# Two layers of a graph network on one core: where the graph attention begins, where its weights are split, and the order of its sums and second scores

## The reference

```python
xn = layernorm(x)
# attention branch, 12 heads of 64: q = elu(q)+1, k = elu(k)+1
attn = q @ k.T ; attn /= sum(attn) ; out = (attn @ v) @ w_proj + b_proj
# graph branch, twice: gat_layer(x, W, att_src, att_dst, bias, heads, out_ch)
h = (x @ W.T).reshape(n, heads, out_ch)
a_src, a_dst = (h * att_src).sum(-1), (h * att_dst).sum(-1)
e = leaky_relu(a_src[src] + a_dst[dst], 0.2)
alpha = softmax of e over the edges that end in the same node
out = segment_sum(alpha * h[src], dst) + bias
# first: 8 heads of 128, then relu; second: 1 head of 768
x = x + graph branch + attention branch
```

## Time and profile before

| | us |
|---|---|
| median of 3 runs | 2029.58 (2028.18 to 2029.92) |
| the profiled execution | 2031.99 |
| its span in the trace | 2030.1 |
| PE busy in the span | 1864.3 (92%) |
| DVE busy | 1307.8 (64%) |
| ACT busy | 907.4 (45%) |
| POOL busy | 154.9 (8%) |
| linear projection | 739.0 to 777.1 |
| graph attention, first product to last sum | 776.8 to 1065.2 |

### The profile page before, as it was taken

One profiled execution on the slowest core, in us unless ns is written; L12 is line 12 of the kernel. 1 busy time (PEld: TensorE's weight loads), 2 busy tenths in 40 slices (PEclk: granted clock), 3 DMA queues, 4 the chain that ended last, 5 costly groups with the idle time before them and its releaser, 6 DMA issues.

```text
span 2030.1 us, 30857 instructions
## 1 busy us (share of the span) xinstructions
PE 1864.3 (92%) x12197; PEld 1769.5 (87%) x12198; DVE 1307.8 (64%) x2466; ACT 907.4 (45%) x1503; POOL 154.9 (8%) x129
## 2 busy tenths in 40 slices
PE   5987999899999996888768999999999999999998
PEld 4875888898889995788667899999999999999998
DVE  6997766545345655987765663446565666666886
ACT  2331222324134433765434223235555665666775
POOL 0000000004000003422110000000101001001010
PEclk9997998999999997888979899999999999999999
DMA  3110002001212202010012112236566657676795
GB/s 114 48 47 1 24 24 102 32 24 49 70 48 86 71 32 96 22 37 16 34 76 97 61 66 101 86 117 220 198 216 199 225 210 243 226 258 236 286 321 197
DMA packets 36796, 234.30 MB, mean 115 GB/s; under 512 B 5916, under 2 KB 7318, under 8 KB 14632
## 3 DMA queue, kind: packets, MB, share of 16 engines
q1 hardware_dynamic: 31318, 217.41, 30.1%
q0 software_dynamic: 2656, 8.99, 2.0%
q10 hardware_dynamic: 2674, 5.87, 0.7%
...
## 4 chain that ended last, share of the span: by engine, by line
PE 74%; DVE 13%; issue 8%; ACT 3%; DMA 2%; POOL 0%; SPq 0%; DVEq 0%; ACTq 0%; POOLq 0%
PE bank L326 16%; PE bank L327 15%; PE bank L328 15%; PE bank L2599 8%; PE bank L650 4%; PE bank L2600 3%; PE bank L2611 3%; DVE weight_lo L299 2%; PE bank L2615 2%; PE bank L2603 2%; PE bank L2612 2%; PE bank L2614 1%; DVE mix_kv L873 1%; PE bank L2602 1%; DVE gat_edge L2243 1%
## 5 line engine op out<-in xcount | busy, mean ns | idle before, releaser
L299 DVE TENSOR_TENSOR weight_lo<-weight_raw,weight_hi 128x2304 fp32r<-128x2304 f32 (+1 forms) x155 | 388.8, 2513 | 38.7 <-ACT weight_hi L289 38.5
L289 ACT ACTIVATE weight_hi<-weight_raw 128x2304 fp32r<-128x2304 f32 (+1 forms) x155 | 323.2, 2087 | 71.6 <-DMA weight_raw<-in_ffn_w 50.4
L326 PE MATMUL bank<-xT_hi,weight_hi 128*128 128x320 f32 (+1 forms) x576 | 182.0, 316 | 2.2 <-DVE xT_lo L347 2.1
L327 PE MATMUL bank<-xT_lo,weight_hi 128*128 128x320 f32 (+1 forms) x576 | 177.5, 308 | 0.0
L328 PE MATMUL bank<-xT_hi,weight_lo 128*128 128x320 f32 (+1 forms) x576 | 177.3, 308 | 0.0
L326 PE MATMUL bank<-weight_hi,xT_hi 128*128 128x384 f32 (+1 forms) x480 | 162.5, 339 | 8.3 <-DVE xT_lo L347 4.8
L2973 DVE TENSOR_TENSOR hidden_tmp<-hidden_tmp,bank 128x160 f32<-128x160 f32 (+5 forms) x192 | 65.6, 341 | 160.8 <-ACT hidden_tmp L2759 160.0
L327 PE MATMUL bank<-weight_lo,xT_hi 128*128 128x384 f32 (+1 forms) x480 | 158.7, 331 | 0.0
L328 PE MATMUL bank<-weight_hi,xT_lo 128*128 128x384 f32 (+1 forms) x480 | 158.5, 330 | 0.0
L650 PE MATMUL bank<-one_hot_dst,one_hot_src 125*128 125x313 f16 x800 | 122.6, 304 | 15.2 <-ACT packed_counts L664 7.9
L2759 ACT ACTIVATE hidden_tmp<-bank,ffn_b_by_load 128x160 f32<-128x160 f32 (+5 forms) x192 | 73.4, 402 | 121.4 <-PE bank L2603 115.2
...
## 6 DMA issues: line engine op xcount, KB each, us to landing
...
```

The lines of the kernel that those rows point to most:

```text
L289: act.activation(upper_, whole_, ACT.Copy).then_inc(*w_hi.one())
L299: dve.tensor_tensor(lower_, whole_, upper_.bitcast(F32), ALU.subtract).then_inc(*w_lo.one())
L326: pe.matmul(dst, a[0], b[0], start=first, stop=False)
L327: pe.matmul(dst, a[0], b[1], start=False, stop=False)
```

## The change

- `normalised_attention` ends after the attends. All ten are made before any projection: group 0's beside the last four query products, group 1's after them. Its output tiles get room for all five node tiles, and turns, projections and their sums are returned as functions (`Projection`) that the graph attention calls.
- `graph_attention` starts when the attends are done (`attended`). In each engine's list the steps of group 0 and the turns, products, halves and sums of the projection alternate. The edge buffers 0 to 4 lie in memory that the attends have freed, 5 and 6 in that of the projection's operands. ACT's wait for the last sum and the store of x stand in tick 5; the projection's halves and sums of the last tiles stand in ticks 2, 3 and 5.
- Of the stage's weights one is split before the loop; six are split one at a time at the end of the ticks 10, 12, 14, 20, 24 and 28 (`SPLIT`). SP loads one weight fewer before the stage.
- On DVE, a tick's sums come behind the lower halves of the turned edges, scaling and peak. Second scores of a pair's first tile follow its sums in the same tick, the second tile's come in the next tick behind these as well. The lower halves of h2 are made after the loop, two ahead of the score rows' lower halves and three behind.

```diff
-        kp = pair("mix1_k", [P, TT, HALF], scope)
-        vp = pair("mix1_v", [P, TT, HG, DO], scope)
...
         inverse = sb("mix1_inverse", [P, 2, HG], F32, scope)
+
+        row2 = sb("mix1_row", [P, (GAT_FIRST - 4 * (2 * PAIRS * (TP + PW) + WORK * HALF + 2 * HG)) // 4], F32, scope)[:, 0:D]
+        kp = pair("mix1_k", [P, TT, HALF], scope)
+
+        with ExitStack() as outs_scope:
+            outs = sb("mix1_out", [P, TT, D], F32, outs_scope)
+        vp = pair("mix1_v", [P, TT, HG, DO], scope)
         blank = work[:, :, :].rearrange("p a n -> p (a n)")[:, 0:PAIRS * PW].rearrange("p (a n) -> p a n", a=PAIRS)
 
...
+        BESIDE = {8: (0,), 9: (1,), 10: (2,), 11: (3, 4)}
 
         def sync():
             sp.wait_ge(*x_ready)
             sp.dma_start(bias0[:, :], spread_row(ins["mix1_b"], D)).then_inc(*row_in.dma())
-            sp.dma_start(outs[:, 0, :], spread_row(ins["gat_b2"], D)).then_inc(*row_in.dma())
-            weights_load(c0 + 8 + DEPTH - 1)
+            sp.dma_start(row2, spread_row(ins["gat_b2"], D)).then_inc(*row_in.dma())
+            weights_load(c0 + 10)
 
...
+                end.then_inc(*o_full.one())
 
             keys(0)
             values(0)
...
             per_head(1)
-            attend(0)
-            attend(1)
-            turn(0)
+            for i in range(8, 12):
+                queries(i)
+                for t in BESIDE[i]:
+                    attend(0, t)
             for t in range(TT):
-                if t + 2 < TT:
-                    attend(t + 2)
-                project(t, 0)
-                if t + 1 < TT:
-                    turn(t + 1)
-                project(t, 1)
+                attend(1, t)
 
 
         def scalar():
...
             biases()
             values(0)
             weights_lo(c0 + 1)
-            queries(0)
+            for i in range(6):
+                queries(i)
             per_head(0)
             weights_lo(c0 + 2)
             keys(1)
             weights_lo(c0 + 3)
             values(1)
             weights_lo(c0 + 4)
...
+        for engine in (act, dve, pool, sp):
+            engine.wait_ge(*projection.attended)
         (x_kept, x_back, b1_in, pick_filled, pick_made, log_made, terms_made, edges_known,
          att_in, h_full, h_hi, h_lo, scored, score_turned, score_hi, score_lo, rows_full, rows_kept,
          e_acted, e_made, e_exp, e_scaled, ex_turned, ex_hi, ex_lo, z_full, z_relu, z_hi, z_lo,
@@ -1843,22 +1855,25 @@
         minus_peak = sb("gat_minus_peak", [P, 2, 2, TT], F32, gat)
         total = sb("gat_total", [P, 2, 2, TT], F32, gat)
         rowT = pair("gat_rowT", [2, TP], gat)
-        hg = [pair(f"gat_h{n}", [P, TT, GW], gat) for n in range(2)]
-        src_row = [sb(f"gat_src_row{n}", [P, 2, TP], F32, gat) for n in range(2)]
...
+        dst_bias = sb("gat_dst_bias", [P, 2, TT, 2], F32, gat)
+        b1 = sb("gat_b1", [P, G1], F32, gat)
+        half_scores = sb("gat2_half_scores", [P, TT, 2, 2], F32, gat)
+        h_first = pair("gat_h0", [P, TT, GW], gat)
+        src_first = sb("gat_src_row0", [P, 2, TP], F32, gat)
+
         ZS, XS = 7, DEPTH
...
 
         PREPARE = {6: (0, 1), 7: (2, 3), 8: (4, "turned"), 9: ("spread",)}
 
+        SPLIT = {10: c0 + 2, 12: c0 + 3, 14: c0 + 4, 20: c0 + 5, 24: c0 + 6, 28: c0 + 7}
+
         def unit(i, lag):
 
...
             sp.dma_start(b1[:, :], ins["gat_b1"]).then_inc(*b1_in.dma())
             for grp in range(4):
                 cols = slice(grp * GW, (grp + 1) * GW)
-                if grp:
-                    sp.wait_ge(*scored.at(TT * grp))
-                else:
-                    sp.wait_ge(*x_ready)
+                sp.wait_ge(*(scored.at(TT * grp) if grp else projection.bias_added))
                 for n, name in enumerate(("gat_as1", "gat_ad1")):
                     sp.dma_start(att[:, n, :], spread_row(ins[name][cols], GW)).then_inc(*att_in.dma())
-                weights_load(c0 + 5 + grp)
+                if grp:
+                    weights_load(c0 + 5 + grp)
             sp.wait_ge(*scored.at(4 * TT))
             sp.wait_ge(*e_acted.at(30))
             sp.wait_ge(*terms_made.at(TT + 30))
...
+            def project(t):
+                projection.project(t, 0)
+                projection.project(t, 1)
+
+            prepare(0, 0)
+            projection.turn(0)
+            prepare(0, 1)
+            prepare(0, 2)
+            projection.turn(1)
+            prepare(0, 3)
+            prepare(0, 4)
+            projection.project(0, 0)
+            prepare(0, "turned")
+            projection.project(0, 1)
+            projection.turn(2)
+            projection.project(1, 0)
+            prepare(0, "spread")
+            projection.project(1, 1)
+            projection.turn(3)
+            project(2)
+            projection.turn(4)
+            project(3)
+            project(4)
             for i in range(N1 + LAST_LAG):
                 q = pair_closing(i, 9)
                 if q is not None and pairs_of[q][1] == 1:
...
 
 
         def scalar():
-            act.activation(edge_log[:, :, :], count[:, :, :], ACT.Ln).then_inc(*log_made.one())
-            act.wait_ge(*x_ready)
-            act.dma_start(slots_dram[:, 0:D].rearrange("(t p) d -> p t d", p=P), x[:, :, :]).then_inc(*x_kept.dma())
-            act.wait_ge(*pick_filled.at(2))
...
                     act.activation(hg[grp % 2][0][:, step, :], h_banks[n][:, 0:GW], ACT.Copy).then_inc(*h_hi.one())
                     if step == TT - 1:
-                        if grp == 0:
-                            weights_hi(c0 - 1)
                         weight_read[w1_chunk(grp)] = h_full.at(TT * (grp + 1))
-                        if grp < 3:
-                            weights_hi(w1_chunk(grp))
 
             def raw_edges(u, grp, h, t):
 
...
 
-            for grp, step in FIRST_STEPS:
-                prepare(grp, step)
+            act.wait_ge(*pick_filled.at(2))
+            act.activation(pick[:, :, :], pick_f, ACT.Copy).then_inc(*pick_made.one())
+            prepare(0, 0)
+            projection.turned_upper(0)
+            prepare(0, 1)
+            prepare(0, 2)
+            projection.turned_upper(1)
+            prepare(0, 3)
+            prepare(0, 4)
+            weights_hi(c0 - 2)
+            act.activation(edge_log[:, :, :], count[:, :, :], ACT.Ln).then_inc(*log_made.one())
+            prepare(0, "turned")
+            projection.turned_upper(2)
+            prepare(0, "spread")
+            act.wait_ge(*b1_in.at(16))
             for i in range(N1 + LAST_LAG + 1):
+                if i == 2:
+                    projection.turned_upper(3)
...
+                    projection.turned_upper(3)
+                if i == 3:
+                    projection.turned_upper(4)
+                if i == 5:
+                    act.wait_ge(*x_ready)
+                    act.dma_start(slots_dram[:, 0:D].rearrange("(t p) d -> p t d", p=P), x[:, :, :]).then_inc(*x_kept.dma())
                 q = pair_closing(i, 8)
                 if q is not None:
...
                     weight_read[w2_chunk(grp)] = y_full.at(10 * (grp + 1))
-                    if grp < 2:
-                        weights_hi(w2_chunk(grp))
...
+                if i in SPLIT:
+                    weight_hi(SPLIT[i])
+                q = pair_closing(i, 10)
+                if q is not None and pairs_of[q][0:2] == (3, 1):
+                    _, _, t0, n = pairs_of[q]
+                    for t in range(t0, t0 + n):
+                        act.wait_ge(*y_added.at(2 * (3 * TT + t) + 2))
+                        if t == 0:
+                            act.wait_ge(*h_full.at(4 * TT))
+                        upper(at(hp, ALL, t, ALL), h2[:, t, :]).then_inc(*h2_hi.one())
             rows_turned(4)
             rows_spread(4)
             for i in range(TT + 6):
...
-                    if step == TT - 1 and grp == 0:
-                        weights_lo(c0 - 1)
-                    if step == TT - 1 and grp < 3:
-                        weights_lo(w1_chunk(grp))
 
             def edge_logs():
...
+            def second_scores(t):
+                dve.wait_ge(*att_in.at(32 * 5))
+                dve.wait_ge(*y_added.at(2 * (3 * TT + t) + 2))
+                for k in range(2):
+                    for c in range(2):
+                        c_ = slice(c * HALF, (c + 1) * HALF)
+                        dve.wait_ge(*dve_own.now())
+                        dot(h2[:, t, c_], att2[k][:, c_], unread2[:, c, 0:HALF], half_scores[:, t, k, c:c + 1],
+                            scored2 if k == 1 and c == 1 else dve_own)
+                dve.wait_ge(*scored2.now())
+
+            def second_lower(t):
+                dve.wait_ge(*h2_hi.at(t + 1))
+                lower(at(hp, ALL, t, ALL), h2[:, t, :]).then_inc(*h2_lo.one())
+
             def turned_lower(u, dst):
...
-            for grp, step in FIRST_STEPS:
-                prepare(grp, step)
+            prepare(0, 0)
+            projection.turned_lower(0)
+            prepare(0, 1)
```

(62 more changed lines are left out.)

247 lines of the change are left out of this document (110 added, 137 removed).

## The result

The changed kernel took 2010.78 us (median of 4 runs, 2008.69 to 2015.20), the kernel before 2029.75 in the same session (4 runs, 2028.18 to 2033.28): ratio 0.9905, 95% interval 0.9885 to 0.9925. It is faster, by 19 us and not by 40.5, and outside the range. The profiled execution took 2008.69 us with a span of 2006.8, so against the old profiled execution (2031.99, 2030.1) the two traces differ by 23.3 us; the 23.3 is what is to be explained here. It is larger than the 19 of the medians because the profiled execution after is the fastest of its four, 2.1 us under their median, and the profiled execution before lies 2.2 us over the median of its kernel.

A forecast was written before the change was run, and what follows sets the result against it. A serial opening on DVE, ACT and POOL stood behind the PE-full projection; afterwards neither PE nor DVE alone was the bound. Gains 21 + 9 + 10.5 = 40.5 us take the median 2029.58 to 1989; range 1978 to 2004.

The forecast's parts named there:

- Step 1: Opening: graph attention's serial start moved beside the projection; DVE starts tick 6 at 796 instead of 817.4, gain 21 us.
- the 1.6 us stall of PE: Opening: PE wants the scores at 757.9, DVE has them at 759.5, so PE loses 1.6 us.
- The cover of 23 us: Opening: PE's projection of tiles 2 to 4, some 23 us, under which ticks 0 to 4 fit.
- C: Opening: score vectors land after 8.5 us and new waits add a few; gain 12 to 14, 1997 us; chance 0.12.
- A: Interleaved projection: PE stops before most tiles and its clock falls, costing 45 us; 2034 us, slower; chance 0.03.
- D: Opening: still waits in some queue for the whole projection, so only the other two steps pay; 2010 us; chance 0.05.
- Step 2: Middle: one split per tick and later sums give back PE's waits; gain 9 us, bounds 14 and -3.5.
- E: Middle: regains all its waits, 14 us, with PE at full clock there; 1980 us; chance 0.08.
- Rival B: Middle: splits at tick ends and late sums delay DVE; -3.5 us instead of +9, 2001.5 us; chance 0.10.
- Step 3: End: scores reordered and lower halves moved shorten PE's two gaps by 6.2 and 4.9 us; gain 10.5 us.
- The first gap: End: PE's 7.73 us wait before the last turned units' lower halves shrinks to 1.5; gain 6.2 us.
- the second: End: PE's 8.67 us gap before 1021.62 shrinks to about 4; gain 4.9 us.

The follow-up runs named there:

- e14: Kernel before; the opening keeps its two splits, the other four made one per tick, DVE halves one tick later behind the lower halves: 2029.8 us.
- e13: Kernel before with only the change's six splits, their DVE halves one tick later, behind the lower halves: 2037.3 us.
- e4: Kernel before with only the change's six splits, last in ticks 10, 12, 14, 20, 24 and 28: 2044.4 us.
- e3: Changed kernel with the sums of groups 0 to 2 put back ahead of the turned edges' lower halves: 2016.7 us.
- e6: Kernel before with only the sums of groups 0 to 2 moved behind the peak of their tick: 2027.4 us.
- e2: Changed kernel with the DVE halves of all six splits one tick later, behind the lower halves: 2003.7 us.
- e5: Changed kernel with its six splits one tick sooner (9, 11, 13, 19, 23, 27), still last in their ticks: 2007.8 us.
- e1: Changed kernel with the DVE halves of five of the six splits moved ahead of the peak of the same tick: 2010.6 us.

## Why the prediction was wrong, step by step

**Step 1, the opening: right.** Forecast 796 for the first turned unit's lower half, measured 795.19. The waypoints:

```profile
745.06 0.56 DVE L1745 TENSOR_TENSOR mix_out<-bank,mix_inverse 114x384 f32<-114x384 f32 x1
...
759.40 0.08 DVE L2234 DVE_READ_ACCUMULATOR2_ANT gat_scores<- 128x1 f32 x1
...
795.19 0.89 DVE L362 TENSOR_TENSOR weight_lo<-bank,weight_hi 128x384 fp32r<-128x384 f32 x2 [0.88 <-ACT weight_hi L359]
```

```profile
793.14 0.83 ACT L2145 ACTIVATE gat_edge<-gat_edge,gat_minus_peak 128x640 f32<-128x640 f32 x1 [9.18 <-DVE x L1825]
```

```profile
746.70 12.06 POOL L1971 TENSOR_SCALAR gat_edge<-edge_count 128x640 f32<-128x640 uint16 x5
...
769.75 1.57 POOL L1980 TENSOR_TENSOR edge_terms<-gat_edge_log,gat_src_row 128x640 f32<-128x640 f32 x1 [10.99 <-DVE gat_has_edge L2275]
```

"Attended" came at 745.6 (745 forecast), the last score at 759.5 (759.5), the logarithm at 759.50 (757), PE's last projection product at 792.1 (792.3); the 1.6 us stall of PE did not come at all, and DVE was busy 0.67 of the time where I had named 0.7. The cover of 23 us held: POOL stood ready at 769.75, 22 us before the projection's end. What ended last was x_ready, as said: ACT's line above waited 9.18 us for DVE's last sum into x. Of the rivals C fell (DVE waited 1.7 us for the score vectors and had them at 749.65, for 749.5 in the forecast), and A fell: the clock was 1.00 throughout, with no gap of PE in it. D fell too, since the opening won its 22.5 us; that its 2010 is the measured time is chance.

**Step 2, the middle: wrong, in sign.** "Gain 9 us" was a loss of 8.7, and the failing step is that of the splits: "less part of one more split per group on a DVE with 9 us of idle time in 52.9". Two things were mis-sized in it, the number of splits in the middle and their place in the tick. One path of middles leads from before to the change over e14, e13, and e4 (e3 stands for e4 at 178.2):

- two splits more, in ticks 10 and 12, behind the lower halves: +7.5 (e13 less e14), where the text took 0.8 off a group for its further split (4.3 to 3.5) and 3.5 for both as its bound;
- the other four one per tick: +0.35 (e14 less before), nothing, right;
- last in their ticks instead of behind: +8.1 (e4 less e13), priced at nothing;
- the later sums: -7.3 (the change less e3).

That these add up to +8.6 for +8.7 measured is no test, since the runs form a chain. The shares depend on the order: over e6 and e2 they are -4.0 for the sums on the old kernel, +7.4 for six splits behind, +5.3 for putting them last. In either order the splits cost more than the sums bring (+15.9 and -7.3, or +12.7 and -4.0). The three waits that the forecast gave back did not all fall either: the turn's 4.7 us went, while those before a product and for scores stayed (6.5 for 6.0, 8.5 for 8.2), and the 11.1 us on the splits came in addition.

The idle time of DVE was real but was no cover: it lies where DVE waits for ACT's copies (9.3 us ahead of the node products' lower halves in the change's middle), once per group, and e13 and e14 recover just there, 3.2 us at the end of group 1, after PE has stopped before it. That this is why two splits more could not be covered is my reading of the peaks; no run moved that idle time. A per-group count of waits and idle time could not see it. And I took 1.75 us for a split from a row where it ran alone, though I had put it right behind a peak, whose end is what releases POOL. The forecast also priced late sums at 2 us in each of 12 ticks "inside the second rival", which has only -3.5 for all, and gave E 14 us where its own waits leave 8.2 + 6.0 + 4.7 - 6.3 = 12.6. Neither decided: the sums gained, and E fell with the middle. Rival B had the right place and half the mechanism ("splits at tick ends and late sums delay DVE"), with a bound of -3.5 that stood on the same 1.75 us; its 2001.5 was nearer, and the late sums were the part of it that was wrong.

**Step 3, the end: right.** 10.5 forecast, 9.0 measured from peak 39 to peak 40, 7.1 alone on the old kernel. The first gap was forecast at 1.5, the second at 4. PE's waits from 960 to 1035, and where they fall:

```profile
PE bank L2026 <- issue: 5.7, 1, 5.7
PE bank L341 <- DVE weight_lo L362: 4.8, 3, 2.8
PE bank L1995 <- DVE gat_scores L2377: 3.4, 1, 3.4
```

```profile
964.60 0.51 PE L341 MATMUL bank<-weight_hi,gat_h_hi 128*128 128x256 f32 x1 [2.80 <-DVE weight_lo L362]
...
978.43 0.39 PE L341 MATMUL bank<-weight_hi,gat_h_hi 128*128 128x256 f32 x1 [1.45 <-DVE weight_lo L362]
981.63 0.33 PE L341 MATMUL bank<-weight_hi,gat_h_hi 128*128 128x128 f32 x1 [0.60 <-DVE weight_lo L362]
...
997.89 1.23 PE L1995 MATMUL bank<-identity,gat_scores 128*1 128x128 f32 x5 [3.35 <-DVE gat_scores L2377]
```

The wait for scores is 3.35 for 8.67, and the lower halves' 7.73 became 1.45 and 0.60; the 2.80 lies ahead of peak 39. The wait of 5.7 before L2026 was there before, with 5.3. Between the two peaks PE stood still for 45.98 - 23.75 = 22.2 us before and 37.01 - 25.27 = 11.7 after: 10.5 less, as forecast. The missing 1.5 is PE's busy time, 25.27 for 23.75, with 12 matmuls more in the stretch (156 for 144): 13 fewer lie in the middle (923 for 936), so at peak 39 PE is further behind DVE than it was.

**The sum.** 22.5 - 8.7 + 9.0 = 22.8, and 0.5 more behind peak 40, against 40.5. Of the 17.7 us that are missing, 17.7 lie in step 2, -1.5 in step 1 and 1.5 in step 3. The range's upper end rested on rivals B and C, and B's loss of 3.5 us in the middle was too small: 8.7 came.

**Port.** I had weighed the port rule for POOL's selects and found that they end before the split. That was so: they ran 746.70 to 758.76, the split started at 759.51 and took 1.76. The contention lay elsewhere, in the edge terms. Four of the change's six splits met one. At 820.48 and 877.21 the term had 1.05 us left and the split took 0.92 over 1.75; at 838.38 and 893.57 it had 1.39 and 1.38 left and the split took 1.26 and 1.25 more. Each was held for all but some 0.13 us of what POOL had left; POOL's terms, which had started first, kept their 1.53 to 1.54. The Trainium skill, page "SBUF — State Buffer", section "Who interferes with whom", holds that the two exclude each other for the whole instruction; by that rule, the trace agrees, and it should have been asked of every POOL instruction beside every moved one. Which of the two loses follows from which starts first. In e4 (as in e3 and e5) one split started 0.22 us ahead of a term; the split kept its 1.75 and the term took 2.92:

```profile
850.99 1.75 DVE L299 TENSOR_TENSOR weight_lo<-weight_raw,weight_hi 128x1536 fp32r<-128x1536 f32 x1
...
851.21 2.92 POOL L1969 TENSOR_TENSOR edge_terms<-gat_edge_log,gat_src_row 128x640 f32<-128x640 f32 x1 [5.09 <-DVE gat_minus_peak L2237]
```

The dots of the opening, which read one operand from PSUM, kept 289 ns beside the selects. How much of the last place's cost is this holding and how much the place ahead of z's lower half was not separated: e1 took the first away and met ACT, e5 took half of both. The holding is 4.4 us in the change (14.9 less 6 x 1.75) and 4.4 in e4. With the sums behind, the last place costs 5.3 us in all, so nearly all of it could be the holding; with the sums ahead it costs 8.1, about twice the holding.
